# Masked keys of four tiles of a shifted-window attention block, copied by transfers of two tiles each

## The reference

```
xn = layernorm over the 64 channels (x)
windows of 8 x 8 of xn, rolled by 4 in height and width: 64 windows of 64 tokens
q, k, v = xn @ in_w.T + in_b,  8 heads of 8 channels
attn = softmax(q k.T / sqrt(8)) v, then out_w, proj_w; roll back
y = x + attn
out = y + fc2(gelu(fc1(layernorm(y))))     hidden 256
```

## Time and profile before

| | |
|---|---|
| median of three runs | 88.35 us (87.68 to 89.39) |
| the profiled execution, its own time | 87.13 us |
| its span, first to last instruction | 85.1 us |
| granted clock of TensorE | 1.00 |
| busy: TensorE / VectorE / ScalarE / GpSimd | 92% / 79% / 59% / 61% of the span |
| masked copies by DMA | 38 of 32 KB, 8 of 64 KB |

### The profile page before, as it was taken

The page is one execution under the profiler, slowest core; times in us unless marked ns, Lnnn a source line. Parts: engine busy times, 40 slices in busy tenths (PEclk is TensorE's granted clock), DMA queues, the critical chain, the costliest instruction groups (busy, mean ns, idle before and its releaser), DMA issues.

```text
span 85.1 us, 3855 instructions
## 1 busy us (share of the span) xinstructions
PE 78.3 (92%) x1578; PEld 44.9 (53%) x1578; DVE 66.9 (79%) x218; ACT 50.2 (59%) x83; POOL 51.9 (61%) x62
## 2 busy tenths in 40 slices
PE   5987999997999999999899998999999999999950
PEld 5974757455766764664565556465454423333420
DVE  4999998989999999989979999999743954333260
ACT  0396898976358756678378347453597755725400
POOL 7988829995593981999694584985817054700000
PEclk9999999999999999999999999999999999999999
DMA  0879710111110111220111210000000000032042
GB/s 12 239 249 434 306 50 0 45 58 32 46 53 30 48 42 46 69 84 17 61 39 49 89 47 23 0 8 0 8 0 8 0 0 0 0 123 87 37 161 85
DMA packets 3488, 5.71 MB, mean 67 GB/s; under 512 B 944, under 2 KB 1712, under 8 KB 3344
## 3 DMA queue, kind: packets, MB, share of 16 engines
q1 hardware_dynamic: 2608, 3.08, 10.6%
q10 hardware_dynamic: 864, 2.40, 7.7%
HBM read 2.66 MB, written 1.05 MB: 44 GB/s over the span
## 4 chain that ended last, share of the span: by engine, by line
PE 50%; DVE 22%; SPq 14%; issue 7%; DMA 2%; ACT 1%; DVEq 0%
SPq L260 10%; PE ps_s L332 8%; PE ps_u L426 6%; PE ps_u L496 5%; DVE row_max L655 4%; SPq L250 4%; PE ps_t L480 3%; PE ps_t L332 3%; PE ps_m L306 3%; DVE stats L635 3%; PE ps_s L480 2%; PE ps_o L496 2%; DMA masked<-qk 2%; DVE masked L831 2%; PE ps_o L440 2%
## 5 line engine op out<-in xcount | busy, mean ns | idle before, releaser
L1050 POOL TENSOR_TENSOR max_x<-max_t,early 128x512 bf16<-128x512 bf16 x14 | 14.7, 1047 | 10.3 <-DVE max_t L668 10.3
L930 ACT ACTIVATE probs<-ps_t 128x1024 f32<-128x1024 f32 x13 | 13.3, 1024 | 9.8 <-PE ps_t L409 9.0
L655 DVE TENSOR_REDUCE row_max<-ps_s 128x16 f32<-128x1024 f32 x15 | 18.0, 1200 | 0.4
L332 PE MATMUL ps_s<-masked,qk 32*64 32x256 f32 x240 | 16.4, 386 | 1.4 <-DVE row_max L655 0.5
L332 PE MATMUL ps_t<-masked,qk 32*64 32x256 f32 x224 | 15.5, 387 | 0.0
L1059 POOL TENSOR_TENSOR rstd<-y_var,minus_half 128x4 f32<-128x4 f32 x8 | 8.3, 1033 | 6.7 <-DVE y_var L718 6.7
L332 PEld LDWEIGHTS ps_s<-masked,qk 32*64 32x64 f32 x240 | 8.3, 131 | 6.1 <-issue 2.5
L426 PE MATMUL ps_u<-probs,vz 128*32 128x64 f32 x512 | 10.5, 222 | 0.0
L426 PEld LDWEIGHTS ps_u<-probs,vz 128*32 128x32 f32 x512 | 7.9, 109 | 3.4 <-issue 3.2
L1035 POOL TENSOR_TENSOR rstd<-var,minus_half 128x4 f32<-128x4 f32 x8 | 8.5, 1062 | 1.0 <-DVE var L643 0.4
L674 DVE STREAM_TRANSPOSE sums<-ps_u 128x512 f32<-128x512 f32 x8 | 5.6, 704 | 3.0 <-PE ps_u L426 3.0
(11 more groups left out here) (112 smaller groups left out, 146.6 us busy)
## 6 DMA issues: line engine op xcount, KB each, us to landing
masked<-qk SPq DMA_DIRECT2D x38, 32.0 KB, 1.8
x_ch<-x_ch_d ACTq DMA_DIRECT2D x1, 1024.0 KB, 8.6
out_d<-result SPq DMA_DIRECT2D x3, 256.0 KB, 2.5
x_tok<-x_tok_d ACTq DMA_DIRECT2D x1, 512.0 KB, 6.5
masked<-qk SPq DMA_DIRECT2D x8, 64.0 KB, 2.5
late<-late_d ACTq DMA_DIRECT2D x1, 352.0 KB, 5.7
x_tok<-x_tok_d SPq DMA_DIRECT2D x2, 128.0 KB, 3.3
x_tok<-x_tok_d ACTq DMA_DIRECT2D x1, 256.0 KB, 5.3
```

The costliest lines, as they stand in the source:

```text
L332: return nc.tensor.matmul(ps[o:o + L, g, n * TOK:(n + 1) * TOK], qk[r:r + RG, b, w, t], masked[r:r + RG, b, :, w, t], start=(n == 0), stop ...
L655: nc.vector.tensor_reduce(row_max[:, w, 0:16], score_bank(k, w)[:].rearrange("q g (h j) -> q (g h) j", j=L), axis=AX.X, op=ALU.max).then_i ...
L930: nc.scalar.activation(probs[:, w, :], scores_t_bank(k, w)[:].rearrange("q g c -> q (g c)"), ACT.Exp).then_inc(probs_done, 1)
L1050: nc.gpsimd.tensor_tensor(max_x[:, k % 2, w, :].rearrange("q (n i) -> q n i", n=16), bf16_high(max_t[:, w, :]).unsqueeze(1).to_broadcast([ ...
```

## The change

The keys of tiles 4 and 5, and of 6 and 7, are copied by four DMAs of two tiles each, as the queries of these tiles were already. The new function waits for the copy of the second tile of the pair, and for the scores (not their shift) of the tiles that had the buffers before. TensorE waits for the pair at the first scores of its even tile and no more at the odd one. The semaphores of the four buffers are now used by tiles 1 to 3 alone.

```diff
+        k_pair_masked = [sem(f"k_pair_masked{i}") for i in range((TILES - QB) // 2)]
...
+            def mask_keys_of_pair(k):
+                b = k % QB
+                sp.wait_ge(qk_copied, k + 2)
+                sp.wait_ge(scores_done, 2 * (k + 1 - QB) + 2)
+                for h in range(SLOTS):
+                    sp.dma_start(masked[h:C:SLOTS, b:b + 2, h], qk[C + h:P:SLOTS, b:b + 2]).then_inc(k_pair_masked[k // 2 - 2], 16)
...
             def mask_heads(k, dst, src, done, heads=SLOTS):
                 b = k % QB
                 sp.wait_ge(qk_copied, k + 1)
-                if k < QB:
-                    sp.wait_ge(masked_zeroed[k], 1)
-                else:
-                    sp.wait_ge(scores_shifted, 2 * (k - QB) + 2)
+                sp.wait_ge(masked_zeroed[k], 1)
...
             for k in range(1, TILES):
-                if k < QB or k % 2 == 0:
-                    mask_heads(k, 0, C, k_masked[k % QB], 2 if k in (1, 2) else SLOTS)
                 if k < QB:
+                    mask_heads(k, 0, C, k_masked[k], 2 if k in (1, 2) else SLOTS)
                     mask_heads(k, C, 0, q_masked[k])
-                elif k % 2:
+                elif k % 2 == 0:
+                    mask_keys_of_pair(k)
+                else:
                     mask_queries_of_pair(k - 1)
-                    mask_heads(k, 0, C, k_masked[k % QB])
...
                 elif w == 0:
-                    pe.wait_ge(k_masked[k % QB], 64 * (k // QB) + (0, 32, 32, 64)[k % QB])
+                    if k < QB:
+                        pe.wait_ge(k_masked[k], (0, 32, 32, 64)[k])
+                    elif k % 2 == 0:
+                        pe.wait_ge(k_pair_masked[k // 2 - 2], 64)
```

## The result

The changed kernel takes **92.11 us**, median of four runs (90.72 to 93.59), against 88.02 before (with a fourth run, of 87.68); the ratio is 1.032 (95% interval 1.022 to 1.043). It is slower. The four runs lie at two levels: 90.7 and 90.8 with a mean granted clock of 1.00, 93.4 and 93.6 with one of 0.96; the ratio is that of the former. The profiled execution is of the former too: 90.72 us, a span of 88.9, where before it was 87.13 and 85.1.

What follows compares the result with a forecast made beforehand. TensorE was taken as the bound, with only 0.35 us to gain from SP's queue. The terms 2.1 - 0.35 + 2.2 - 0.4 = 3.55 us on the 88.35 median gave 91.9 us, range 89.7 to 93.2.

Steps and rivals of the forecast that it cites:

- The mechanism: Ahead of slots 3 and 5: joined keys wait for the second tile's copy, land late, and TensorE stands for them.
- First stop: Ahead of slot 3: TensorE waits for keys 4 and 5, 2.1 us lost, bounds 1.5 and 2.7.
- Slot 3 gave back: Ahead of slot 4: TensorE's wait for tile 5's keys goes, 0.35 us back.
- the rule that TensorE's idle time is all that can be won: In the slots behind the stops: only TensorE's idle time can come back, 0.36 and 0.38 us.
- Second stop: Ahead of slot 5: TensorE waits for keys 6 and 7, 2.2 us lost, bounds 1.8 and 3.1.
- Slot 5 gave back: In slot 5: VectorE catches up during the stop, so TensorE's waits on it go, 0.4 us back, ends 0 and 0.4.
- the last rival, TensorE's clock: In the stops: the clock falls, and a slot at 1.2 GHz adds up to its 6.1 busy us; chance 2%.
- Fewer issues: On SP's queue: eight issues fewer free SP, so not slower; 88.0 us at best, 89.5 with shortest landings; chance 7%.
- The landing that decides: Ahead of slot 3: for no loss the fourth pair of keys must land by 35.15, 0.9 us after its issue.
- Half of the loss: In the slots behind the stops: VectorE catches up and half is won back, giving 90.1 us; chance 10%.
- issue among keys 6 and 7: Ahead of slot 5: the fourth issue meets the instruction transfer and is stretched, 0.9 us more, 92.8 us; chance 14%.
- the estimate of 2.15 us for a pair's landing: For a 64 KB pair: about 2.0 us fixed plus bytes at 436 GB/s; by it the whole sum would be 2.1 us.

Runs made afterwards that it cites:

- the single pairs: Kernel before with only one pair of keys joined: tiles 4 and 5 took 89.6, 89.9, 88.0 and 89.6 us; tiles 6 and 7 took 90.0 to 90.6.

## Why the prediction was right

**The mechanism** was right, and its times close: issues of keys 4 and 5 at 32.29, 32.93, 33.57 and 34.21 were forecast, and 32.30, 33.57 and 34.21 stand above for the first, third and fourth. The fourth was stretched by the instruction transfer as forecast and slot 3 began at 37.35, forecast 37.25. That the wait and not the size costs is shown from both sides: by the kernel that has only the wait, for slot 3, and by the one that has only the pair, for both slots.

**The sizes.** First stop 2.2 us (forecast 2.1). Slot 3 gave back 0.65 us (0.35): beside the wait for keys 5 there are 0.3 us that the prediction held to be impossible there, by the rule that TensorE's idle time is all that can be won. That step failed, because part of TensorE's waiting does not stand in its idle time. TensorE's weight loads (PEld), before and after, show it:

```profile
40.06 0.20 PEld L466 LDWEIGHTS ps_m<-ident_sb,rstd_x 128*128 128x128 f32 x2 [0.25 <-POOL rstd_x L1066]
...
41.98 0.25 PEld L474 LDWEIGHTS ps_m<-ident_sb,rstd_x 128*128 128x128 f32 x2
```

Before, the load of rstd_x waited 0.25 us for GpSimd, which ended it at 39.15 + 0.86 = 40.01, while the products ahead of it still counted as busy. In the changed kernel GpSimd ends it at the same time, 40.02, but slot 3 has moved by 2.2 us and finds it done. So GpSimd used the stop to go on with slot 3's work on its own list, which the prediction had ruled out: from the products ahead of this load to those behind it TensorE is 0.2 us faster. The last 0.1 us is the end of the slot, where the next scores now start while the last products still run. Second stop 2.45 us (2.2), since its last pair needed 3.0 us to land, not 2.8. Slot 5 gave back 0.19 (0.4): the wait on VectorE ahead of slot 6 stayed, at 0.24. The sum over the spans is 3.8, the forecast's 3.55.

**What was wrong** is the last rival, TensorE's clock, at 2%. I argued from the clock after TensorE's last product that a stop does it nothing. Of the eight runs of the changed kernel five had a mean clock between 0.96 and 0.98. They took 1.6 to 3.1 us more than the runs at 1.00 beside them, 1.3 to 2.0 for each stop if the clock fell there once at 0.98 and twice at 0.96, as the traces of the single pairs suggest; none of the five has a trace of its own. That 91.9 us lies so near the median of 92.11 is therefore luck: no run took that time, and the median falls between two runs at 1.00 and two at 0.96. At a clock of 1.00 the change costs 2.9 us by the ratio and 3.6 by the two profiled executions, and the rest of the 4.1 us between the medians goes with the clock. The forecast came to nearly the same time by putting its 3.55 us on the median of 88.35 rather than on the profiled 87.13.

**The other rivals.** Fewer issues went with 0.7 us less where nothing waits for the second tile, but so did a better order of as many issues as before. The landing that decides came 3.1 us after its issue and not 0.9. Half of the loss was not absorbed: 0.3 and 0.2 us were. No issue among keys 6 and 7 was stretched by 0.9 us; the fourth took 0.59, and its landing alone was late. As to the estimate of 2.15 us for a pair's landing by the Trainium skill ("DMA: Bandwidth & Descriptors", the section "Anatomy of one DMA — SWDGE (gpsimd) path"): the section is on transfers that GpSimd issues, and these are issued by SP; the median of the sixteen pairs is 2.2, near the estimate and nearer than the 2.4 that I took for an undisturbed one. But the two landings on which TensorE waited took 3.1 and 3.0.

## What to carry to other kernels

Before joining transfers, look for who needs the first half first: joined, it leaves when the second half is ready, and here that was 2.9 us before it was needed, with four issues and a landing still to come. In this kernel joining was right where the consumer comes late (queries), and the full queue was better cured by the order of what is in it. The last landing before a deadline is to be priced as a disturbed one, 3 us here and not the median of 2. And an engine that counts as busy may still wait: read its weight loads too, before calling a stretch without idle time full.

## What the runs showed of the hardware

Issues of masked copies mostly take 0.5 to 0.6 us. In the twelve traces each one over 0.8 us (up to 1.96) has a transfer of queue 8 ("instruction", 16 KB) that begins between 0.42 us ahead of its start and 0.21 us behind it, and lands 2.2 to 3.3 us after its start. Two issues met such a transfer and kept their length; issues into which one begins later, 0.3 us or more behind their start, kept theirs too but landed after 2.5 to 3.4 us. The transfers come, 12 or 13 in an execution, whether SP issues or not: in the changed kernel one begins at 30.19, while SP stands. In the changed kernel the issue at 34.21 met one as that at 34.32 had before. Where such a transfer falls shifts from run to run (the sixth at 37.97 and at 38.81 in the two traces of the kernel before), and with it the key that is late.

Stops of 2.2 to 2.5 us of TensorE within its work, and one of 1.61, are followed by a stretch at 1.2 GHz in some traces and not in others, with the same kernel; it costs some 1.4 us. With six products of zeros in the stop, into a PSUM bank that is free anyway, none of twelve runs had a mean clock under 0.995; without them twelve of sixteen were at 0.96 to 0.98. The stops are not the only occasion: the clock also fell where TensorE had only 0.5 us of idle time.
